# A new order for the same instructions: masked-tile pieces, engine queues and SyncE's queue of a four-layer graph network

## The reference, cut to what matters

```python
x = norm(x + adj @ (x @ W0) + b0)                              # layer 0
res = si[:, :, None] + sj[:, None, :] + adj * w_r + g_b        # layer 1: rank one terms and adj
x = norm(x + einsum('bij,bjd->bid', res, x) @ W1 + b1)
e = sigmoid(a_tgt[:, :, None] + a_src[:, None, :] + be) * mask # layer 2: attention, 1024 x 1024 a batch
x = norm(x + layer2(e @ x_h, x_h * e.sum(-1)))
for _ in range(5):                                             # layer 3: a gated step, five times
    m = adj @ h
    z, r = sigmoid(gates(m, h)); hv = tanh(W5 m + U5 (r * h)); h = (1 - z) * h + z * hv
x = norm(x + h)
```

## Time and profile before

| | |
|---|---|
| median of 3 runs | 1240.87 us (1238.55 to 1243.62) |
| the profiled execution: its own time, its span | 1239.06 us, 1237.2 us |
| PE busy | 1173.9 us (95% of the span) |
| DVE, ACT, POOL busy | 927.3, 690.7, 73.8 us |
| mean granted clock of TensorE | 0.987 |

### The profile page before, as it was taken

The page is one execution under the profiler, slowest core; times in us unless marked ns, Lnnn a source line. Parts: engine busy times, 40 slices in busy tenths (PEclk is TensorE's granted clock), DMA queues, the critical chain, the costliest instruction groups (busy, mean ns, idle before and its releaser), DMA issues.

```text
span 1237.2 us, 15533 instructions
## 1 busy us (share of the span) xinstructions
PE 1173.9 (95%) x5232; PEld 909.8 (74%) x5232; DVE 927.3 (75%) x2071; ACT 690.7 (56%) x1125; POOL 73.8 (6%) x80
## 2 busy tenths in 40 slices
...
PEclk9999899899999999999999999999999999999997
...
GB/s 249 151 12 80 87 141 1 46 100 94 110 87 94 77 94 84 36 69 86 77 85 80 101 150 37 81 66 33 86 119 100 117 56 85 18 1 1 1 0 35
DMA packets 92575, 93.66 MB, mean 76 GB/s; under 512 B 9104, under 2 KB 62992, under 8 KB 92496
## 3 DMA queue, kind: packets, MB, share of 16 engines
...
q0 software_dynamic: 144, 0.40, 0.2%
...
## 4 chain that ended last, share of the span: by engine, by line
PE 66%; DVE 16%; ACT 6%; SPq 4%; issue 3%; DMA 3%; POOL 1%; DVEq 0%; POOLq 0%; ACTq 0%
PE ps L812 37%; PE ps L817 5%; PE ps L819 5%; PE ps L818 5%; PE ps L935 4%; PE ps L830 3%; ACT x L1132 2%; DVE ring L1543 2%; SPq L692 1%; PE ps L823 1%; DVE hT L1597 1%; DVE tl L1358 1%; DVE v L1594 1%; DVE ml L1358 1%; PE ps L879 1%
## 5 line engine op out<-in xcount | busy, mean ns | idle before, releaser
L812 PE MATMUL ps<-adj_hi,xh 128*128 128x512 f32 x672 | 286.8, 427 | 14.2 <-DVE ml L1358 8.4
L812 PE MATMUL ps<-adj_hi,xl 128*128 128x512 f32 x672 | 264.1, 393 | 0.0
L812 PE MATMUL ps<-adj_lo,xh 128*128 128x512 f32 x672 | 263.7, 392 | 0.0
L812 PEld LDWEIGHTS ps<-adj_hi,xh 128*128 128x128 f32 x672 | 127.3, 190 | 53.6 <-issue 24.2
L812 PEld LDWEIGHTS ps<-adj_lo,xh 128*128 128x128 f32 x672 | 127.5, 190 | 34.8 <-issue 11.0
L812 PEld LDWEIGHTS ps<-adj_hi,xl 128*128 128x128 f32 x672 | 127.1, 189 | 27.6
L1127 ACT ACTIVATE mh<-ps 128x512 fp32r<-128x512 f32 x80 | 47.2, 590 | 108.6 <-PE ps L812 108.6
L817 PE MATMUL ps<-mh,wh 128*128 128x512 f32 x240 | 100.2, 418 | 5.8 <-DVE ml L1358 4.4
L1205 ACT ACTIVATE ring<-fh,asn 128x512 f32<-128x512 f32 x96 | 66.9, 718 | 61.6 <-PE ps L935 25.3
L1576 DVE TENSOR_TENSOR r<-r,hT 128x512 f32<-128x512 f32 x80 | 53.2, 687 | 61.6 <-ACT r L1270 61.6
L1543 DVE TENSOR_TENSOR ring<-ring,mk 128x512 f32<-128x512 f32 x128 | 86.9, 683 | 13.1 <-ACT ring L1205 12.1
...
## 6 DMA issues: line engine op xcount, KB each, us to landing
mk<-mask_scratch SPq DMA_DIRECT2D x128, 256.0 KB, 2.8
state_scratch<-v SPq DMA_DIRECT2D x60, 256.0 KB, 2.0
...
layer_scratch<-fk SPq DMA_DIRECT2D x12, 256.0 KB, 2.2
...
fh<-target_scratch SPq DMA_DIRECT2D x12, 256.0 KB, 3.3
```

Of the source, the lines that this page charges most:

```text
L812: mm = pe.matmul(dst, a[:, t, :], b[:, t, cut(h)], start=(t == 0 and i == 0), stop=(t == T - 1 and i == 2))
```

## The change

Nothing but the four large tables changes: SP, PE, ACT and DVE. Each holds the same pieces, and POOL's table, all functions, buffers and banks stay. Cut to its core:

```diff
     "SP": """
-first k01:1 k02:1 ... k10:1 k11:1 t2a:2 t2b:2 k12:1 f2a:2 f2b:2 k13:1 k14:1 k15:1
-first k16:1 k17:1 k00:2 k01:2 k02:2 ax:2 tga:2 tgb:2
+first k01:1 k02:1 ... k14:1 k15:1 t2a:2 t2b:2 f2a:2 k16:1
+first k17:1 f2b:2 k00:2 k01:2 k02:2 ax:2 tga:2 tgb:2 k03:2
-unit14 @3 k03:4 @5 k04:4 k05:4 k06:4 k07:4 k10:4
-unit15 @3 k11:4 @4 k12:4 @5 k13:4
+unit14 @5 k03:4 k04:4 ... k14:4 k15:4
-unit20 @1 k15:5 k16:5 k17:5 k00:6 k01:6 k02:6
+unit20
     "PE": """
-first tgb:1 rvb:0 m0a:3 e00:1 y2b:0 e01:1 e02:1 e03:1 m0b:3 e04:1 e05:1 e06:1 e07:1 y0a:3 y0b:3
-unit0 @1 e10:1 e11:1 @2 e12:1 @3 e13:1 e14:1 @4 e15:1 @5 e16:1 e17:1 @7 rsa:1 @8 pja:2 rsb:1 @12 rva:1 ...
-unit1 @22 e00:2 e01:2 e02:2
-unit2 @12 e03:2 @18 e04:2 @19 e05:2 @21 e06:2 @24 rsa:2
+first rvb:0 e00:1 ... e06:1 y2b:0 e07:1 m0a:3 e10:1 e11:1 e12:1 m0b:3 e13:1 e14:1
+first e15:1 e16:1 y0a:3 e17:1 y0b:3 rsa:1 pja:2 pjb:2
+unit0 @2 rsb:1 @5 rva:1 @8 m1a:3 rvb:1 m1b:3 y2a:1 sums:3 y2b:1 rows:3 y1a:3 th0:2 @11 y1b:3 @12 th1:2 @20 th2:2
+unit1 @9 e00:2 @22 e01:2 e02:2 e03:2
+unit2 @4 e04:2 @9 e05:2 @19 rsa:2 e06:2 e07:2 @21 rva:2 @23 e10:2 @25 y2a:2
-unit20 @1 rva:5 @3 e10:5 ... @19 e16:5 e17:5 rsb:5 @21 rvb:5 m0a:6 y2b:5 m0b:6 @25 y0a:6 y0b:6
-unit21 @22 m1a:6
+unit19 @1 e07:5 rsa:5 @8 e10:5 e11:5 e12:5 rva:5 ... e17:5 rsb:5 @16 rvb:5 @22 y2b:5
+unit20 @21 m0a:6 @26 m0b:6
+unit21 @1 y0a:6 @3 y0b:6 @22 m1a:6 @24 m1b:6
     "ACT": """
-first ... n0:2 pja:0 pjb:0 tha:0 thb:0 tga:0 ...
+first ... pja:0 pjb:0 n0:2 tha:0 thb:0 tga:0 n1:1 tgb:0 ...
-unit0 @0 ... @4 n0:3 rva:1 pja:2 m1a:3 m1b:3 rvb:1 pjb:2 @9 n2:1 @11 th0:2
+unit0 @0 ... @1 n0:3 @2 rva:1 @4 m1a:3 rvb:1 m1b:3 th0:2 th1:2 n2:1 @9 n1:3 @11 th2:2
-unit1 @0 n1:3 th1:2 th2:2 @6 s00:2 s01:2 s02:2 q00:2 q01:2 s03:2 ...
+unit1 @1 s00:2 s01:2 @2 q00:2 s02:2 q01:2 @6 s03:2 ...
     "DVE": """
-first x0:0 c0:0 x0:1 x0:2 y0a:0 c0:1 y0b:0 weights:0 v0:0 mask:0 ...
+first x0:0 x0:1 weights:0 c0:1 c0:0 mask:0 x0:2 y0a:0 y0b:0 mask:1 v0:0 ...
-unit29 @1 s17:7 @3 y2a:7 @4 rsb:7 @5 rvb:7 @9 y2b:7 @10 v2:7
+unit29 @4 rva:7 s13:7 s14:7 y2a:7 s15:7 s16:7 s17:7 rsb:7 @5 rvb:7 @11 y2b:7 @15 v2:7
```

More of the change, by code:

```diff
@@ L82 @@
[L82 to L86 removed]
+first m0a:0 m0b:0 m0a:1 y0a:0 y0b:0 m0b:1 y0a:1 y0b:1 m0a:2 m0b:2 m1a:0 m1b:0 sums:0 m1a:1 rows:0 y1a:0
@@ new lines @@
+first m1b:1 y1b:0 sums:1 y0a:2 y0b:2 rows:1 y1a:1 y1b:1 t2a:0 t2b:0 pja:0 pjb:0 tha:0 thb:0 tga:0 tgb:0
+first m1a:2 e00:0 e01:0 e02:0 t2a:1 e03:0 m1b:2 e04:0 e05:0 t2b:1 e06:0 e07:0 pja:1 rsa:0 sums:2 rva:0 e10:0
+first e11:0 e12:0 y2a:0 pjb:1 e13:0 e14:0 e15:0 rows:2 y1a:2 tha:1 thb:1 y1b:2 tga:1 e16:0 tgb:1 e17:0 rsb:0
+first rvb:0 e00:1 e01:1 e02:1 e03:1 e04:1 e05:1 e06:1 y2b:0 e07:1 m0a:3 e10:1 e11:1 e12:1 m0b:3 e13:1 e14:1
+first e15:1 e16:1 y0a:3 e17:1 y0b:3 rsa:1 pja:2 pjb:2
+unit0 @2 rsb:1 @5 rva:1 @8 m1a:3 rvb:1 m1b:3 y2a:1 sums:3 y2b:1 rows:3 y1a:3 th0:2 @11 y1b:3 @12 th1:2 @20 th2:2
@@ L92 @@
+unit7 @10 e03:3 @17 e04:3 e05:3 @19 e06:3 @26 rsa:3
+unit8 @4 e07:3 @5 rva:3 @11 y2a:3 e10:3 @17 e11:3 @18 e12:3 @21 e13:3
+unit9 @4 e14:3 @10 e15:3 @16 e16:3 rsb:3 e17:3 @17 rvb:3 @22 y2b:3
 unit10 @21 m0a:4 @26 m0b:4
[L93 to L98, removed]
@@ L107 @@
[L107 to L111, removed]
+unit11 @1 y0a:4 @3 y0b:4 @22 m1a:4 @24 m1b:4 @26 sums:4
@@ new lines @@
+unit12 @15 rows:4 @21 y1a:4 @22 y1b:4
+unit13 @19 m0a:5 @22 m0b:5 pja:4 y0a:5 pjb:4 @23 y0b:5 @26 th0:4 th1:4
+unit14 @3 th2:4 @11 m1a:5 @18 m1b:5 e00:4 sums:5 e01:4 e02:4 e03:4 @21 e04:4 e05:4 rows:5 @22 e06:4
+unit15 @8 e07:4 y1a:5 rsa:4 @12 e10:4 e11:4 e12:4 rva:4 @22 y1b:5 e13:4
+unit16 @2 e14:4 y2a:4 e15:4 e16:4 @10 e17:4 rsb:4 @15 rvb:4 @22 y2b:4
+unit17 @13 pja:5 pjb:5 @21 th0:5 th1:5 @23 th2:5
+unit18 @12 e00:5 @17 e01:5 @18 e02:5 @19 e03:5 @25 e04:5 @26 e05:5 e06:5
+unit19 @1 e07:5 rsa:5 @8 e10:5 e11:5 e12:5 rva:5 e13:5 @9 e14:5 @10 e15:5 @11 y2a:5 @14 e16:5 @15 e17:5 rsb:5 @16 rvb:5 @22 y2b:5
```

174 lines of the change are left out of this document (88 added, 86 removed).

## The result

The changed kernel takes 1236.53 us, median of 6 runs (1235.14 to 1238.19), against 1240.99 us for the kernel before in the same comparison: a ratio of 0.9962, 95% interval [0.9946, 0.9978]. That is 4.5 us less: clear of no change by the interval, and less than the 0.5% from which this text calls a kernel faster. The forecast was 1235.3 us and "same" the likeliest class. Its profiled execution took 1235.95 us, span 1234.0 us.

A forecast was written before the change was run, and what follows sets the result against it. PE, busy 95% of the span, was taken as the bound, so only its idle and half-clock time could move. Terms -2.4 - 0.9 - 2.2 - 0.4 + 0.5 - 0.2 = -5.6 us gave a 1235.3 us median, range 1228 to 1244.

The forecast's parts named there:

- Unit 30: Pair change at unit 30: moving `v2:7` shrinks PE's pause from 3.21 towards 0.82 us; -2.4 us, bounds 0 and -3.2.
- Half clock behind it: Units 30 and 31: with one of two long pauses gone, half of 1.8 us is saved; -0.9 us, bounds 0 and -1.8.
- Units 20 and 21 with 12 to 19: Three pauses become one, -3.2 us; denser units 12 to 19 cost +1.0; sum -2.2, bounds 0 and -4.
- Units 22 to 29: Re-ordered only; mask loads behind state transfers let a state's second half be fetched sooner; -0.4 us, bounds +2 and -1.
- Start and unit 0: Before unit 1: eleven more products precede unit 0, gains and losses nearly cancel; +0.5 us, bounds -5 and +5.
- units 1 to 9: Unit 1 net +0.6 us, units 2 to 9 -0.8; together -0.2 us, bounds +6 and -4.
- The walk: Both orders followed to unit 1's start: 228.4 against 227.97 us, good to 4 us.
- The wait for `mk`: Unit 1: a 2 us wait at batch 2's first tile, ahead of the second product, was named as a sign.
- Rival D: Before unit 1: idle time becomes one piece, half clock follows, up to 14 us lost; slower, 1249 us, chance 0.11.
- e00:2: Piece of batch 2 at PE's opening 9 of unit 1, waiting for the target row: PE stands 2 us, before 0.57.
- Rival C: Units 17 to 19 and 27 to 29: PE waits for DVE, taking back the pair changes' gains; 1240.5 us, chance 0.25.
- Rival B: Start and units 1 to 9: half of DVE's 6 us lead reaches PE, another 7 us go; 1228 us, chance 0.16.

The follow-up runs named there:

- v2_7_late: The kernel before with one DVE piece, `v2:7`, moved from opening 10 of unit 29 to opening 15: 1237.39 us, ratio 0.9969.
- out_late: The changed kernel with pair 2's last output normalisation on ACT moved to the next unit, behind the split and the two candidates: 1234.49 us, 0.9949.
- only_A: The kernel before with the changed kernel's orders ahead of unit 0 and in units 0 to 9 alone: 1244.34 us, ratio 1.0016.
- filled: The changed kernel with 28 extra matmuls of constants in PE's idle time before unit 1's first product: 1240.94 us, 0.9994 of the kernel before.
- filled_12: The changed kernel with 12 extra matmuls of constants in PE's idle time before unit 1's first product: 1238.65 us, 0.9977 of the kernel before.

## Why the prediction was right, and where it was not

The class and the size were right: -5.6 us forecast, -4.5 measured. The largest term and its mechanism were right as well; that the sum came so near is in part luck, since the other terms were off by about 1 us each, two too small a gain and two too large. The terms, each against profiles of kernels with the same orders up to the place:

*Unit 30, -2.4 us.* Right in mechanism and size: pause 3.21 to 0.82, `reset_hi`'s idle time gone, the unit 22.1 to 19.7 us. v2_7_late shows it as the cause, alone. What is late next was said to be `n2:7`; it is `v2:7` itself, in opening 15 ahead of `ml`, together with the output norm (out_late).

*Half clock behind it, -0.9.* Mis-sized, and put to one place where there are several. Units 30 and 31 take 44.9, 46.3 and 46.5 us in the three profiles with both pauses (half clock once, twice and twice), and 40.9, 40.9, 42.5, 42.5, 42.4 and 42.5 in six with the first pause gone. The means are 45.9 and 41.9: -4.0, where the two terms say -3.3. The profile that the forecast was made against was a lucky one; in it half clock came once. The prediction read from the first matmul of 0.47 us behind 3.21 us of idling that half clock had not followed; in unit 30 that was so, but unit 31 shows the same 0.47 with half clock behind it.

*Units 20 and 21 with 12 to 19, -3.2 + 1.0.* The pauses went as said: three to one of 0.82 us. The price of the denser units 12 to 19 was undersized: idle time in units 10 to 19 rose from 1.3 to 3.7 us, by 2.4, spread over six units, of which the largest is 1.08 at 676. It is not the wait for DVE beyond 2 us that was named as a refutation; it is many waits under 1.1, the largest for ACT. Over all the profiles, units 10 to 22 take 374.2 us with the old orders, or 375.8 where half clock follows unit 21 (three and two of five), and 372.4 to 374.8 with the new ones (mean of nine 373.5): -1.4 against means of 374.8, where -2.2 was said. Here too the gain is in part half clock that can no longer come.

*Units 22 to 29, -0.4.* From unit 23 to 29 -0.7 in the pair of profiles; ten profiles with the new orders have a mean of 204.6 us, four with the old ones 205.9 (v2_7_late counted with these). The sign held, and -1.3 is three times the term. Which of the edits there gives it is not tested.

*Start and unit 0, +0.5; units 1 to 9, -0.2.* Under-priced. The start of unit 10 moved by +1.6 in the pair of profiles. Six profiles with the old orders have it at 444.7 to 447.3 (mean 445.9), three with the new ones at 446.3, 446.6 and 446.9 (mean 446.6): +0.7, within the spread of the six, and only_A measures 0.16%, 2 us [0.4, 3.7]. The walk had unit 0 at 176.5 and unit 1 at 228.4; the trace has 179.3 and 230.8. What it missed, 2.8 us, lies before unit 0. The 3.09 us at `tga:0` are not it: the walk had that wait, at 4 us. One that it does not name is the largest behind it, at the tile `e03:1` (timelines of DVE and PE, the changed kernel):

```profile
144.62 1.65 DVE L1367 BATCH_NORM_STATS2 stAp<-x 128x6 f32<-128x128 f32 x8
```

```profile
147.79 1.12 PE L945 MATMUL ps<-ring,fm 128*128 128x512 f32 x2 [2.52 <-DVE ring L1544]
```

DVE's new order has the statistics `v1:2` ahead of `s03:1`, and PE's order has nothing between `e02:1` and `e03:1` to cover it: the form of `v2:7` once more, made anew by the change (in the kernel before `v1:2` stands at 131.25, and PE's wait for the next tile is 0.42 us). The wait is 2.5 us in six of the eight profiles with this start and 0.82 in the two others; no run moves the piece, so its price is not measured. The wait for `mk` at the first tile of batch 2, said to be 2 us, did not come in the changed kernel: unit 1 itself came 2.4 us late, and its product slow. In filled, with the product at full clock, it is there (1.78 us).

*Rival D* was right on the form and wrong on the price. The idle time before unit 1 is one piece, 7.07 us, half clock follows, and `e00:2` stands behind the product. But filled shows what half clock is worth there, nothing: the chain to `e00:2` runs beside it. Half clock came behind the 3.09 us at `tga:0` too (a granted clock of 0.50 in the 4 us from 93.42 on), yet before unit 0 the mean is 0.97 in both kernels, so the new order only has it at other places. The Trainium skill, "TensorE: Matmul & The Clock Gate", section "HAM oscillation — how this bites in real kernels", has PE fall to half rate again each time it is made to idle long. The runs agree for 7.07, 5.45 and 6.97 us, each followed by a first matmul of 0.79 or 0.80 us; for filled_12's 4.36 us, with a mean clock of 0.57 behind it; and for filled, where only 0.73 us were left idle and the clock was 1.00. For pauses of 1.9 to 3.2 us one and the same order went both ways. That page counts the half rate as lost; here it was lost behind the pauses of units 21, 30 and 31 and free in unit 1.

*Rival C's mechanism* was real: it took back 2.4 of the 3.1 us idle time gained in units 20 and 21. It did not decide, since unit 30 has no such price. *Rival B* fell: nothing of the start's 37 us came back.
